# Self-attention scores of a head pair as alternating 64-row products, with the projections issued in halves

## The chip, the core and the metric

The kernel runs on one core of a Trainium2 chip. The metric is the device time of one execution in microseconds (us), median of three runs. Engine names are those of the profile: PE is the matrix engine (PEld its weight loads, which can overlap its products), DVE the vector engine, ACT the scalar (activation) engine, POOL and SP the general and the DMA-issuing engine. PSUM is the accumulator memory of PE, 8 banks of 128 rows by 512 fp32 numbers.

## What is computed

A decoder layer on x of 8 batches of 512 tokens by 512: a windowed self-attention with 16 heads of 64, then a cross-attention, then a routed feed-forward block. Only the first part is touched by the change. Its core in the reference is:

```python
def proj(w):
    return jnp.einsum('bsd,de->bse', h, w).reshape(B, S, H, HD).transpose(0, 2, 1, 3)
q, k, v = (proj(w_q), proj(w_k), proj(w_v))
...
ll = jnp.einsum('bhnqd,bhnkd->bhnqk', qw, kw) * scale
cm = jnp.tril(jnp.ones((W, W), bool))
ll = jnp.where(cm, ll, NEG).reshape(B, H, S, W)
...
attn = jax.nn.softmax(jnp.concatenate([ll, lg], axis=-1), axis=-1)
```

The kernel handles one window of 512 tokens (one batch) at a time. The extra "gathered" keys of the reference are the same tokens again, so they enter as a weight of 1 or 2 on each value row (`twice`).

## The kernel before

**Precision.** Projections and scores need more than one fp32r product can give, so each operand is split into a high part (rounded to fp32r) and a low part (the rest), and a product is high x high + low x high + high x low. For the projections that is `product` (L577, L578, L579), three 128-row products of 512 columns for each of four chunks `c`, so 12 for one q or k of a head pair.

**Tiles of a head pair.** A pair p holds two heads: head 0 in rows 0 to 63, head 1 in rows 64 to 127 of the projection's bank. Before the change q goes into `q_both` and k into `k_twice` and `k_lo`. For each head, `q_both` has the high part of q in the head's own 64 rows and the low part in the other 64 rows; `k_twice` has the high part of k in both halves. So one 128-row product (L661, L659) does high x high and low x high at once, and one 64-row product with `k_lo` (L664, L657) adds the third term. A product with a bf16 identity (L665) adds the causal mask to the diagonal 128 columns.

**Units.** A pair's scores fall into five units (`unit_blocks`), each of 512 columns: u=0 and u=1 are the query tile 3 (512 keys) of head 0 and head 1; u=2 and u=3 are query tiles 0 and 2 (128 and 384 keys) of either head; u=4 is query tile 1 (256 keys) of both heads. Unit number i is 5p + u, 40 in a batch. Unit i of the scores is written to `s_bank[i % 2]`.

**Life of a unit.** PE computes the scores ("s"). DVE takes the row maximum (`nmax`, L530, L525). ACT takes the exponential into `probs` (L405) and counts `p_ready`. PE transposes the 128x128 blocks ("t", L673). DVE copies them to `probs_t` (L538). PE multiplies by the values ("pv", L688, eight recorded products of 65 columns). DVE divides by the sum (L552, L553) into `o_norm`. After a pair, "ot" (L697) transposes `o_norm`, and ACT copies it to `o_t`.

**What sets the order.** One list, `attention_plan`, is walked by every engine in the same order, and each engine does in order the steps in which it has work. In step g, before the change, the list holds s(g), t(g-2), pv(g-3), and for u = 0 to 3 one of q, q_lo, k, k_lo of the next pair: "q" and "k" are the projection on PE and the high copy on ACT; "q_lo" and "k_lo" are the subtraction on DVE. Some steps carry work for the next batch on DVE: "stats" (g = 5), "dot" (g = 14), "rank" (g = 22, 24, 27, 29). Engines wait for each other through counting semaphores. PE's scores of unit i wait only for the exponential of unit i-2, which freed its bank:

```python
if i >= 2:
    pe.wait_ge(p_ready, b * NU + i - 1)
```

The eight batches are a hardware loop. Values (v) are projected first in each batch, eight times 12 products, and the last two of them stand behind the first pair's q and k to cover their copies. The last pair of a batch has no next pair to project.

Of the kernel before, what the change touches and what calls it, by code (L numbers as in the profile page):

```python
# [18 lines left out]
F32 = mybir.dt.float32  # L19
# [9 lines left out]
P = 128  # L29
# [49 lines left out]

def head_rows(h):  # L80

    return slice(HD * h, HD * h + HD)


def attention_plan():
# [7 lines left out]
    plan = [("v", i) for i in range(2 * TT - 2)] + [("q", 0), ("q_lo", 0), ("k", 0), ("k_lo", 0)]  # L93
    plan += [("v", i) for i in range(2 * TT - 2, 2 * TT)]
    for g in range(NU + 7):
        p, u = divmod(g, UNITS)
        if g < NU:
            plan.append(("s", g))
# [4 lines left out]
        if g < NU and p + 1 < NPAIR and u < 4:  # L103
            plan.append((("q", "q_lo", "k", "k_lo")[u], p + 1))
# [22 lines left out]
def self_attention(nc, x, norm_w, w_q, w_k, w_v, w_out, scorer_w, scorer_b, x1):  # L127
# [3 lines left out]
    with ExitStack() as ctx:  # L131
# [17 lines left out]
        q_both, k_twice = sb("q_both", [P, 2, 2, S], F32R), sb("k_twice", [P, 2, 2, S], F32R)  # L149
        k_lo = sb("k_lo", [P, 2, S], F32R)  # L150
# [42 lines left out]
        s_ready, s_half = sem("s_ready"), sem("s_half")  # L193
# [24 lines left out]
        def taken(eng, b, key):  # L218
# [139 lines left out]
        def _(act):  # L358
# [16 lines left out]
            with act.Fori(0, B) as b:  # L375
                for kind, i in plan:
# [21 lines left out]
                    if kind == "s":  # L398
# [5 lines left out]
                        for n, (_, _, c0, nk) in enumerate(unit_blocks(i % UNITS)):  # L404
                            ins = nc.scalar.activation(probs[:, i % 2, c0:c0 + nk], s_bank[i % 2][:, c0:c0 + nk],  # L405
# [10 lines left out]
        def _(dv):  # L416
# [83 lines left out]
            with dv.Fori(0, B) as b, done.loop(b, 2 * TT + 2 * TT + 1 + NU, B):  # L500
                for kind, i in plan:
# [6 lines left out]
                    if kind in ("q_lo", "k_lo"):  # L508
                        slot, _ = pj(b, (kind[0], i))
                        dv.wait_ge(qk_hi, b * (2 * NPAIR) + 2 * i + (1 if kind == "q_lo" else 2))  # L510
                        for h in range(2):
                            own, other = head_rows(h), head_rows(1 - h)
                            if kind == "q_lo":
                                ins = nc.vector.scalar_tensor_tensor(q_both[other, i % 2, h, :], pj_bank[slot][own, :],  # L514
                                                                     HD ** -0.5, q_both[own, i % 2, h, :].bitcast(F32),
                                                                     ALU.mult, ALU.subtract)
                            else:
                                ins = nc.vector.tensor_tensor(k_lo[own, i % 2, :], pj_bank[slot][own, :],
                                                              k_twice[own, i % 2, h, :].bitcast(F32), ALU.subtract)
                        ins.then_inc(qk_lo, 1)  # L520
                    if kind == "s":
                        dv.wait_ge(s_ready, b * NU + i + 1)
                        blocks = unit_blocks(i % UNITS)
                        if i % UNITS == UNITS - 1:
                            ins = nc.vector.tensor_reduce(nmax[:, i % 4, :],  # L525
                                                          s_bank[i % 2][:, :].rearrange("p (h k) -> p h k", h=2),
                                                          AX.X, ALU.max, negate=True)
                        else:
                            for n, (_, _, c0, nk) in enumerate(blocks):
                                ins = nc.vector.tensor_reduce(nmax[:, i % 4, n:n + 1], s_bank[i % 2][:, c0:c0 + nk],  # L530
                                                              AX.X, ALU.max, negate=True)
# [42 lines left out]
        def _(pe):  # L574
# [46 lines left out]
            with pe.Fori(0, B) as b:  # L621
                for kind, i in plan:
# [13 lines left out]
                    if kind in ("q", "k"):  # L636
                        slot, _ = pj(b, (kind, i))
                        pe.wait_ge(split_lo, 4 if i < NPAIR // 2 else 6)
                        pj_empty(b, (kind, i))
                        for c in range(DC):  # L640
                            ins = product(pj_bank[slot][:, :], w_hi[kind][:, c, P * i:P * i + P],
                                          w_lo[kind][:, c, P * i:P * i + P], ht_hi[:, c, :], ht_lo[:, c, :],
                                          c == 0, c == DC - 1)
                        ins.then_inc(pj_ready, 1)
                    if kind == "s":
                        p, u = divmod(i, UNITS)
                        slot = i % 2
                        if u == 0:
                            pe.wait_ge(qk_lo, b * (2 * NPAIR) + 2 * p + 2)
                        if i >= 2:  # L650
                            pe.wait_ge(p_ready, b * NU + i - 1)
                        for h, t, c0, nk in unit_blocks(u):
                            queries, rows = slice(P * t, P * t + P), head_rows(h)
# [1108 lines left out]
```

## Time and profile before

| what | value |
|---|---|
| runs | 2414.29, 2414.99, 2419.1 us; median 2414.99 |
| span of the profiled execution | 2414.0 us (the runs add at least 0.3 us around it) |
| PE busy | 2241.6 us, 93% of the span |
| DVE busy | 1349.6 us, 56% |
| ACT busy | 845.5 us, 35% |
| self-attention | about the first 1650 us, eight batches of some 201 us |

The span runs from the first to the last recorded instruction; it is the number against which sums are made. Busy time of PE is modelled: a recorded product of 512 columns lasts 0.39 us while the next one starts 0.23 us after it, so the cost of a product is read from the start of one to the start of the next.

### The profile page before, as it was taken

To read this page: it belongs to the slowest core of one execution; us is meant where nothing else is said; L and a number is where in the kernel's file an instruction comes from. 1 tells how busy PE (TensorE), PEld (TensorE's weight loads), DVE (VectorE), ACT (ScalarE), POOL (GpSimd) and SP (SyncE) were. 2 spreads that over 40 slices of the span, in tenths; PEclk is the share of its full clock that TensorE was granted. 3 is DMA by queue.
4 is the path that set the end of the run, shared out by engine and by line. 5 is a ranking of instruction groups with operands and counts; after the bars stand their busy time and mean duration, and the time that the engine had idled before them with its cause. 6 is when DMAs were issued, how large, how long until landed. Compare 5 with 4: busy or idle time off the path is not lost. (4 is left out here: it accounts for less than half of the span.)

```text
span 2414.0 us, 35686 instructions
## 1 busy us (share of the span) xinstructions
PE 2241.6 (93%) x12029; PEld 1682.4 (70%) x12029; DVE 1349.6 (56%) x3145; ACT 845.5 (35%) x1541; POOL 429.2 (18%) x669
## 2 busy tenths in 40 slices
PE   3999999999999999999999999996898888878899
PEld 3786777678678677767767767773787888865543
DVE  4574376177257437617725743661787878845500
ACT  3442344144144234314414423441644444413210
POOL 2100000010010000001001000002866666620000
PEclk9999999999999999999999999997988888858999
DMA  5000000100100000010010000002013211141000
GB/s 183 1 1 31 23 1 10 45 1 1 54 1 1 31 23 1 10 45 1 1 54 1 1 28 27 1 10 91 29 56 102 83 55 55 53 152 50 1 0 18
DMA packets 46136, 80.23 MB, mean 33 GB/s; under 512 B 10067, under 2 KB 10067, under 8 KB 45448
## 3 DMA queue, kind: packets, MB, share of 16 engines
q1 hardware_dynamic: 45320, 75.85, 9.3%
q8 instruction: 103, 1.69, 0.3%
q0 software_dynamic: 640, 2.10, 0.2%
q14 instruction: 73, 0.60, 0.1%
HBM read 60.11 MB, written 17.83 MB: 32 GB/s over the span
## 5 line engine op out<-in xcount | busy, mean ns | idle before, releaser
L405 ACT ACTIVATE probs<-s_bank,nmax 128x512 f32<-128x512 f32 (+3 forms) x512 | 249.4, 525 | 421.6 <-DVE nmax L530 294.3
L530 DVE TENSOR_REDUCE nmax<-s_bank 128x1 f32<-128x512 f32 (+2 forms) x384 | 185.3, 510 | 305.7 <-PE s_bank L665 302.0
L688 PE MATMUL o_bank<-vals,probs_t 128*128 128x65 f32 x2560 | 322.2, 269 | 0.0
L688 PEld LDWEIGHTS o_bank<-vals,probs_t 128*128 128x128 f32 x2560 | 311.0, 192 | 1.4 <-DVE probs_t L538 1.4
L712 PE MATMUL pj_bank<-w_o,o_t 128*128 128x512 f32 x512 | 223.5, 597 | 6.0 <-ACT o_t L413 6.0
L538 DVE COPY probs_t<-pt_bank 128x512 f32<-128x512 f32 x320 | 218.0, 681 | 3.6 <-PE pt_bank L673 3.6
L319 POOL TENSOR_TENSOR idle<-ones 128x4 f32<-128x4 f32 x41 | 8.1, 198 | 1065.7 <-DMA probs<-in_x 1063.7
L673 PE MATMUL pt_bank<-ident,probs 128*128 128x128 f32 x1280 | 194.1, 274 | 0.0
L712 PEld LDWEIGHTS pj_bank<-w_o,o_t 128*128 128x128 f32 x512 | 97.2, 191 | 127.6 <-issue 127.6
L664 PE MATMUL s_bank<-k_lo,q_both 64*128 64x512 f32 (+3 forms) x448 | 184.9, 413 | 0.0
L514 DVE SCALAR_TENSOR_TENSOR q_both<-pj_bank,q_both 64x512 fp32r<-64x512 f32 x128 | 88.2, 689 | 141.6 <-ACT q_both L392 138.9
L661 PE MATMUL s_bank<-k_twice,q_both 128*128 128x512 f32 (+3 forms) x448 | 166.9, 373 | 0.0
L383 ACT ACTIVATE vals<-pj_bank,twice 128x512 f32<-128x512 f32 x64 | 43.9, 688 | 341.8 <-PE pj_bank L579 336.5
L1259 PEld LDWEIGHTS x_o_bank<-vx,p_t 77*128 77x128 f32 x1024 | 148.9, 224 | 17.2 <-issue 10.0
L1259 PE MATMUL x_o_bank<-vx,p_t 77*128 77x33 f32 x1024 | 143.8, 300 | 3.9 <-DVE att L1141 3.9
L570 DVE TENSOR_TENSOR probs<-pj_bank,probs 128x512 f32<-128x512 f32 x32 | 22.1, 692 | 213.8 <-PE pj_bank L712 195.3
L664 PEld LDWEIGHTS s_bank<-k_lo,q_both 64*128 64x128 f32 x448 | 81.9, 183 | 85.5 <-issue 72.1
L673 PEld LDWEIGHTS pt_bank<-ident,probs 128*128 128x128 f32 x1280 | 135.7, 141 | 0.0
L577 PE MATMUL pj_bank<-wv_hi,ht_hi 128*128 128x512 f32 x256 | 104.2, 407 | 22.9 <-ACT vals L383 9.9
L1245 PE MATMUL e_bank<-qk_bd,xl_t 128*128 128x308 f32 x256 | 96.9, 510 | 27.7 <-DVE e L1123 27.0
L1022 POOL TENSOR_TENSOR e<-e,fill 128x616 f32<-128x616 f32 x64 | 95.3, 1489 | 127.1 <-DVE fill L1129 126.9
L665 PE MATMUL s_bank<-causal_b,ident_b 128*128 128x128 bf16 x512 | 117.7, 230 | 0.0
(266 smaller groups left out, 4245.5 us busy)
## 6 DMA issues: line engine op xcount, KB each, us to landing
xb<-in_x SPq DMA_DIRECT2D x9, 1024.0 KB, 5.3
xt<-x SPq DMA_DIRECT2D x36, 256.0 KB, 2.8
probs<-in_x SPq DMA_DIRECT2D x32, 256.0 KB, 2.7
x<-probs SPq DMA_DIRECT2D x32, 256.0 KB, 2.0
am<-in_L_ffn_attention_mask SPq DMA_DIRECT2D x8, 1024.0 KB, 5.2
out<-x SPq DMA_DIRECT2D x32, 256.0 KB, 2.1
w_sb<-in_L_ffn_w SPq DMA_DIRECT2D x2, 4096.0 KB, 20.2
o_t<-in_L_attn_w_v SPq DMA_DIRECT2D x2, 1024.0 KB, 9.5
```

The source lines that it names most:

```text
L405: ins = nc.scalar.activation(probs[:, i % 2, c0:c0 + nk], s_bank[i % 2][:, c0:c0 + nk], ACT.Exp, bias=nmax[:, i % 4, n:n + 1])
L530: ins = nc.vector.tensor_reduce(nmax[:, i % 4, n:n + 1], s_bank[i % 2][:, c0:c0 + nk], AX.X, ALU.max, negate=True)
L538: nc.vector.tensor_copy(probs_t[:, i % 2, :], pt_bank[slot][:, :]).then_inc(ts_ready, 1)
L577: nc.tensor.matmul(out, lhs_hi, rhs_hi, start=start, stop=False)
L661: nc.tensor.matmul(s_bank[slot][:, c0:c0 + nk], *high, start=True, stop=False)
L664: nc.tensor.matmul(s_bank[slot][:, c0:c0 + nk], *low, start=False, stop=False)
L665: ins = nc.tensor.matmul(s_bank[slot][:, c0 + nk - P:c0 + nk], ident_b[:, :], causal_b[:, :], start=False, stop=True)
L673: ins = nc.tensor.transpose(pt_bank[slot][:, P * j:P * j + P], probs[:, i % 2, P * j:P * j + P], ident[:, :])
L688: ins = nc.tensor.matmul(o_bank[slot][:, o0:o0 + VW], probs_t[:, i % 2, c0 + P * kt:c0 + P * kt + P], vals[:, kt, 2 * p + h, :], start=(kt ...
L712: ins = nc.tensor.matmul(pj_bank[slot][:, :], o_t[:, c, P * i:P * i + P], w_o[:, c, :], start=(c == 0), stop=(c == NPAIR - 1))
L1245: ins = nc.tensor.matmul(e_bank[:, c, 0:CH * SK], xl_t[:, (i // 2) % 2, P * k:P * k + P], qk_bd[:, n.par, k].rearrange("p h k -> p (h k)") ...
L1259: ins = nc.tensor.matmul(o_bank[:, VX * h:VX * h + VX], p_t[:, i % 2, h // CH, P * (h % CH):P * (h % CH) + P], vx[:, n.par, 2 * CH * (i % ...
```

## The change

The plain tiles `q_hi`, `q_lo`, `k_hi`, `k_lo` (both heads in their own 64 rows) replace `q_both` and `k_twice`. One copy of 128 rows on ACT and one subtraction of 128 rows on DVE replace the 64-row ones (for q two and two, for k four and two). The scores become three 64-row products for each block and head (high x high, low x high, high x low). They are issued in turn for head 0 (rows 0 to 63, into `s_bank[0]`) and head 1 (rows 64 to 127, into `s_bank[1]`). A step "rows" does the scores of two units at once (j=0: units u=0, 1; j=1: u=2, 3), or of unit 4 (j=2), and waits until both banks are free. The projections of the next pair are issued as four steps of six products.

```diff
+def row_blocks(j):
+
+    return [[(3, 0, 512)], [(0, 0, 128), (2, 128, 384)], [(1, 0, 256)]][j]
...
     for g in range(NU + 7):
         p, u = divmod(g, UNITS)
-        if g < NU:
-            plan.append(("s", g))
+        more = g < NU and p + 1 < NPAIR
         if 2 <= g < NU + 2:
             plan.append(("t", g - 2))
         if 3 <= g < NU + 3:
             plan.append(("pv", g - 3))
-        if g < NU and p + 1 < NPAIR and u < 4:
-            plan.append((("q", "q_lo", "k", "k_lo")[u], p + 1))
+        if g < NU and u in (0, 2):
+            plan.append(("rows", 3 * p + u // 2))
+        if more and u == 3:
+            plan.append(("k", p + 1))
+        if g < NU and u == 3:
+            plan.append(("rows", 3 * p + 2))
+        if g < NU:
+            plan.append(("s", g))
+        if more and u < 3:
+            plan.append((("q_half", "q", "k_half")[u], p + 1))
+        if more and u == 2:
+            plan.append(("q_lo", p + 1))
+        if more and u == 4:
+            plan.append(("k_lo", p + 1))
...
+        def scores(i, n, c0, nk):
+
+            if i % UNITS == UNITS - 1:
+                return s_bank[n][:, 0:nk]
+            return s_bank[i % UNITS % 2][:, c0:c0 + nk]
...
-                        for h in range(2):
-                            own, other = head_rows(h), head_rows(1 - h)
-                            if kind == "q":
-                                ins = nc.scalar.activation(q_both[own, i % 2, h, :], pj_bank[slot][own, :], ACT.Copy,
-                                                           scale=HD ** -0.5)
-                            else:
-                                nc.scalar.copy(k_twice[own, i % 2, h, :], pj_bank[slot][own, :])
-                                ins = nc.scalar.copy(k_twice[other, i % 2, h, :], pj_bank[slot][own, :])
-                        ins.then_inc(qk_hi, 1)
+                        if kind == "q":
+                            nc.scalar.activation(q_hi[:, i % 2, :], pj_bank[slot][:, :], ACT.Copy,
+                                                 scale=HD ** -0.5).then_inc(qk_hi, 1)
+                        else:
+                            nc.scalar.copy(k_hi[:, i % 2, :], pj_bank[slot][:, :]).then_inc(qk_hi, 1)
...
+                    if kind in ("q_half", "q", "k_half", "k"):
+                        of = kind[0]
+                        slot, _ = pj(b, (of, i))
+                        if kind == of:
+                            chunks = range(DC // 2, DC)
+                        else:
+                            chunks = range(DC // 2)
...
+                    if kind == "rows":
+                        p, j = divmod(i, 3)
+                        first = UNITS * p + 2 * j
+                        if j == 0:
                             pe.wait_ge(qk_lo, b * (2 * NPAIR) + 2 * p + 2)
...
+                        if first:
+                            pe.wait_ge(p_ready, b * NU + first)
+                        blocks = row_blocks(j)
+                        terms = ((q_hi, k_hi), (q_lo, k_hi), (q_hi, k_lo))
+                        for n, (t, c0, nk) in enumerate(blocks):
+                            for m, (queries, keys) in enumerate(terms):
+                                for h in range(2):
+                                    nc.tensor.matmul(s_bank[h][:, c0:c0 + nk],
+                                                     queries[head_rows(h), p % 2, P * t:P * t + P],
+                                                     keys[head_rows(h), p % 2, 0:nk],
+                                                     start=(n == 0 and m == 0), stop=False, skip_group_check=True)
+                        for h in range(2):
+                            for n, (t, c0, nk) in enumerate(blocks):
+                                ins = nc.tensor.matmul(s_bank[h][:, c0 + nk - P:c0 + nk], ident_b[:, :],
+                                                       causal_b[:, :], start=False, stop=(n == len(blocks) - 1),
+                                                       skip_group_check=True)
+                            if j < 2 or h == 1:
+                                ins.then_inc(s_ready, 1)
```

**PE, before, in the middle of a pair**, from the last products of k's projection (L577 to L579) over unit u=3 to its t and pv (line numbers of the kernel before):

```order
L577 MATMUL pj_bank<-ht_hi,wk_hi 128x512
L578 MATMUL pj_bank<-ht_hi,wk_lo 128x512
L579 MATMUL pj_bank<-ht_lo,wk_hi 128x512
L651 REGISTER_ALU
L661 MATMUL s_bank<-k_twice,q_both 128x128 [waits p_ready]
L664 MATMUL s_bank<-k_lo,q_both 128x128
L665 MATMUL s_bank<-causal_b,ident_b 128x128
L661 MATMUL s_bank<-k_twice,q_both 128x384
L664 MATMUL s_bank<-k_lo,q_both 128x384
L665 MATMUL s_bank<-causal_b,ident_b 128x128
L673 MATMUL pt_bank<-ident,probs 128x128 [waits ts_ready,p_ready]
L673 MATMUL pt_bank<-ident,probs 128x128 x3
```

The same place of the change, with its own line numbers: L586 to L588 are `product`, L672 the 64-row products, L678 the mask, L688 the transposes.

```order
L586 MATMUL pj_bank<-ht_hi,wk_hi 128x512
L587 MATMUL pj_bank<-ht_hi,wk_lo 128x512
L588 MATMUL pj_bank<-ht_lo,wk_hi 128x512
L666 REGISTER_ALU
L672 MATMUL s_bank<-k_hi,q_hi 128x256 [waits p_ready]
L672 MATMUL s_bank<-k_hi,q_hi 128x256
L672 MATMUL s_bank<-k_hi,q_lo 128x256 x2
L672 MATMUL s_bank<-k_lo,q_hi 128x256 x2
L678 MATMUL s_bank<-causal_b,ident_b 128x128 x2
L685 REGISTER_ALU
L688 MATMUL pt_bank<-ident,probs 128x128 [waits ts_ready,p_ready]
L688 MATMUL pt_bank<-ident,probs 128x128 x3
```

What stood behind k's projection was unit 5p+3, whose bank the exponential of 5p+1 had freed; now it is unit 5p+4, which needs both banks, so it waits for the exponential of 5p+3.

**ACT, before, at the same place**: the copies of k (L395, L396), then the exponentials of unit 5p+3 (L405, 128 and 384 columns).

```order
L395 CAST k_twice<-pj_bank 64x512 [waits pj_ready]
L396 CAST k_twice<-pj_bank 64x512
L395 CAST k_twice<-pj_bank 64x512
L396 CAST k_twice<-pj_bank 64x512
L399 REGISTER_ALU
L403 REGISTER_ALU [waits max_ready]
L405 ACTIVATE probs<-s_bank,nmax 128x128 [waits pt_ready]
L405 ACTIVATE probs<-s_bank,nmax 128x384
```

And in the change (L415 is the copy of k, L423 the exponential):

```order
L410 REGISTER_ALU
L415 CAST k_hi<-pj_bank 128x512 [waits pj_ready]
L417 REGISTER_ALU
L421 REGISTER_ALU [waits max_ready]
L423 ACTIVATE probs<-s_bank,nmax 128x128 [waits pt_ready]
L423 ACTIVATE probs<-s_bank,nmax 128x384
```

The four copies became one; its place ahead of the exponentials of unit 5p+3 is the same as before.

**DVE, in the change, around unit 5p+4**: the copy of a transposed unit (L547), the division (L561, L562), then the maxima of unit 5p+4 (L539, 256 columns from either bank) and the low part of k (L533).

```order
L544 REGISTER_ALU
L547 COPY probs_t<-pt_bank 128x512 [waits pv_ready,pt_ready]
L561 RECIPROCAL o_rden<-o_bank 128x1 [waits pv_ready]
L65 REGISTER_ALU
L562 TENSOR_TENSOR o_norm<-o_bank,o_rden 128x64 [waits dve_step]
L537 REGISTER_ALU
L539 TENSOR_REDUCE nmax<-s_bank 128x1 [waits s_ready]
L539 TENSOR_REDUCE nmax<-s_bank 128x1
L528 REGISTER_ALU
L533 TENSOR_TENSOR k_lo<-pj_bank,k_hi 128x512 [waits qk_hi]
```

Before the change a step's maximum stood ahead of its copy and division; now t(g-2) and pv(g-3) of the step come first, and the maxima of unit g behind them.

## Rows read from the trace of the kernel before

**Rows 1.** The page, busy time of PE, share of the span, instructions.

```profile
PE 2241.6 (93%) x12029; PEld 1682.4 (70%) x12029; DVE 1349.6 (56%) x3145; ACT 845.5 (35%) x1541; POOL 429.2 (18%) x669
```

**Rows 2.** Busy time in one pair's 18 us of self-attention (window; length, engines; clock).

```profile
321.00:339.00 18.00, 18.00 (x113) 14.34 (x113) 13.98 (x35) 7.84 (x16) 0.00 (x0) 1.00 0.01 1
```

**Rows 3.** Timeline of PE, one pair: start, duration, line, operation, tiles, count.

```profile
508.53 0.48 PE L661 MATMUL s_bank<-k_twice,q_both 128*128 128x512 f32 x1
508.94 0.49 PE L664 MATMUL s_bank<-k_lo,q_both 64*128 64x512 f32 x1
509.37 0.23 PE L665 MATMUL s_bank<-causal_b,ident_b 128*128 128x128 bf16 x1
509.44 0.61 PE L673 MATMUL pt_bank<-ident,probs 128*128 128x128 f32 x4
509.88 1.00 PE L688 MATMUL o_bank<-vals,probs_t 128*128 128x65 f32 x8
510.69 0.48 PE L577 MATMUL pj_bank<-ht_hi,wq_hi 128*128 128x512 f32 x1
...
513.54 0.39 PE L661 MATMUL s_bank<-k_twice,q_both 128*128 128x512 f32 x1
...
514.35 0.61 PE L673 MATMUL pt_bank<-ident,probs 128*128 128x128 f32 x4
...
515.60 0.31 PE L661 MATMUL s_bank<-k_twice,q_both 128*128 128x128 f32 x1
...
516.92 0.61 PE L673 MATMUL pt_bank<-ident,probs 128*128 128x128 f32 x4
...
521.03 0.22 PE L661 MATMUL s_bank<-k_twice,q_both 128*128 128x128 f32 x1
...
522.25 0.61 PE L673 MATMUL pt_bank<-ident,probs 128*128 128x128 f32 x4
...
523.63 0.38 PE L657 MATMUL s_bank<-k_lo,q_both 64*128 64x256 f32 x1
...
524.88 0.60 PE L673 MATMUL pt_bank<-ident,probs 128*128 128x128 f32 x4
...
526.53 0.48 PE L661 MATMUL s_bank<-k_twice,q_both 128*128 128x512 f32 x1
```

**Rows 4.** Timeline of ACT in the same pair.

```profile
518.65 0.84 ACT L405 ACTIVATE probs<-s_bank,nmax 128x128 f32<-128x128 f32 x2 [2.61 <-DVE nmax L530]
521.23 0.58 ACT L395 CAST k_twice<-pj_bank 64x512 fp32r<-64x512 f32 x1 [1.74 <-PE pj_bank L579]
```

**Rows 5.** Timeline of DVE in the same pair.

```profile
509.63 0.69 DVE L530 TENSOR_REDUCE nmax<-s_bank 128x1 f32<-128x512 f32 x1 [0.51 <-PE s_bank L665]
...
517.78 0.76 DVE L530 TENSOR_REDUCE nmax<-s_bank 128x1 f32<-128x128 f32 x2
...
523.83 0.17 DVE L552 RECIPROCAL o_rden<-o_bank 128x1 f32<-128x1 f32 x1
524.03 0.23 DVE L553 TENSOR_TENSOR o_norm<-o_bank,o_rden 128x64 f32<-128x64 f32 x1
524.17 1.38 DVE L518 TENSOR_TENSOR k_lo<-pj_bank,k_twice 64x512 fp32r<-64x512 f32 x2
```

**Rows 6.** Timeline of DVE, the step "stats" in another pair.

```profile
292.34 2.46 DVE L426 BATCH_NORM_STATS2 bn<-xb 128x6 f32<-128x512 f32 x4
```

**Rows 7.** Waits of PE: total us, times, longest.

```profile
PE pj_bank L577 <- DVE k_lo L518: 6.9, 8, 0.9
```

**Rows 8.** Two idle times of PE in the cross-attention (timeline), and windows around them.

```profile
1727.28 1.10 PE L1252 MATMUL x_pt_bank<-x_ident,e 128*77 128x128 f32 x8 [1.32 <-ACT e L1077]
1748.51 0.63 PE L1238 MATMUL t_bank<-x_ident,xl 128*128 128x128 f32 x4 [2.22 <-ACT vx L1058]
...
1726.00:1732.00 6.00, 4.72 (x39) 4.45 (x40) 4.97 (x12) 4.22 (x8) 5.76 (x9) 1.00 0.15 46
1750.00:1753.00 3.00, 3.00 (x12) 2.28 (x10) 0.74 (x3) 2.38 (x4) 1.26 (x5) 0.53 0.00 0
```

More of the change, by code:

```diff
@@ L85, in attention_plan @@
 def attention_plan():
-    plan = [("v", i) for i in range(2 * TT - 2)] + [("q", 0), ("q_lo", 0), ("k", 0), ("k_lo", 0)]
+    plan = [("v", i) for i in range(2 * TT - 2)]
+    plan += [("q_half", 0), ("q", 0), ("q_lo", 0), ("k_half", 0), ("k", 0), ("k_lo", 0)]
     plan += [("v", i) for i in range(2 * TT - 2, 2 * TT)]
@@ L146, in self_attention @@
         vals = sb("vals", [P, TT, H, VW])
-        q_both, k_twice = sb("q_both", [P, 2, 2, S], F32R), sb("k_twice", [P, 2, 2, S], F32R)
-        k_lo = sb("k_lo", [P, 2, S], F32R)
+        q_hi, q_lo, k_hi, k_lo = (sb(n, [P, 2, S], F32R) for n in ("q_hi", "q_lo", "k_hi", "k_lo"))
         probs = sb("probs", [P, 2, 512])
@@ L192, in self_attention @@
         v_ready, v_sum_ready, qk_hi, qk_lo = sem("v_ready"), sem("v_sum_ready"), sem("qk_hi"), sem("qk_lo")
-        s_ready, s_half = sem("s_ready"), sem("s_half")
+        s_ready = sem("s_ready")
         max_ready, p_ready = sem("max_ready"), sem("p_ready")
@@ L404, in _ @@
                         for n, (_, _, c0, nk) in enumerate(unit_blocks(i % UNITS)):
-                            ins = nc.scalar.activation(probs[:, i % 2, c0:c0 + nk], s_bank[i % 2][:, c0:c0 + nk],
+                            ins = nc.scalar.activation(probs[:, i % 2, c0:c0 + nk], scores(i, n, c0, nk),
                                                        ACT.Exp, bias=nmax[:, i % 4, n:n + 1])
@@ L510, in _ @@
                         dv.wait_ge(qk_hi, b * (2 * NPAIR) + 2 * i + (1 if kind == "q_lo" else 2))
[L511 to L519, printed above, removed]
+                        if kind == "q_lo":
+                            ins = nc.vector.scalar_tensor_tensor(q_lo[:, i % 2, :], pj_bank[slot][:, :], HD ** -0.5,
+                                                                 q_hi[:, i % 2, :].bitcast(F32), ALU.mult, ALU.subtract)
+                        else:
+                            ins = nc.vector.tensor_tensor(k_lo[:, i % 2, :], pj_bank[slot][:, :],
+                                                          k_hi[:, i % 2, :].bitcast(F32), ALU.subtract)
                         ins.then_inc(qk_lo, 1)
@@ L522, in _ @@
                         dv.wait_ge(s_ready, b * NU + i + 1)
[L523 to L526, printed above, removed]
+                        for n, (_, _, c0, nk) in enumerate(unit_blocks(i % UNITS)):
+                            ins = nc.vector.tensor_reduce(nmax[:, i % 4, n:n + 1], scores(i, n, c0, nk),
                                                           AX.X, ALU.max, negate=True)
[L528 to L531, printed above, removed]
                         ins.then_inc(max_ready, 1)
@@ L635, in _ @@
                         ins.then_inc(pj_ready, 1)
[L636 to L642, printed above, removed]
-                                          c == 0, c == DC - 1)
-                        ins.then_inc(pj_ready, 1)
@@ new lines, in _ @@
+                    if kind in ("q_half", "q", "k_half", "k"):
[3 more added lines that the diff above has]
+                            chunks = range(DC // 2, DC)
+                        else:
+                            chunks = range(DC // 2)
+                            pe.wait_ge(split_lo, 4 if i < NPAIR // 2 else 6)
+                            pj_empty(b, (of, i))
+                        for c in chunks:
+                            ins = product(pj_bank[slot][:, :], w_hi[of][:, c, P * i:P * i + P],
+                                          w_lo[of][:, c, P * i:P * i + P], ht_hi[:, c, :], ht_lo[:, c, :],
+                                          c == 0, c == DC - 1)
+                        if kind == of:
+                            ins.then_inc(pj_ready, 1)
```

22 lines of the change are left out of this document (removed).

## The prediction

> **What bounds the kernel now.** I read the page first: PE is busy 93% of the span, DVE 56%, ACT 35% [rows 1]. Then the windows: in a pair's 18 us of self-attention PE is busy all 18.00, DVE 13.98, ACT 7.84, at the full clock [rows 2]. So PE sets the time there, and DVE and ACT have slack on average. Then PE's timeline of one pair, from one unit u=0 to the next: 508.53 to 526.53 is 18.00 us [rows 3]. What the change must be judged by is therefore two things: how much PE time the scores lose, and whether the new order makes PE wait, which it does not do now.
>
> **What the scores cost PE now.** From a unit's first product to the next transposes [rows 3]: u=0 takes 0.91 us (508.53 to 509.44), u=1 0.81, u=2 1.32, u=3 1.22, u=4 1.25, together 5.51 us a pair. Much of that is not streaming. Twelve projection products take 2.85 us (510.69 to 513.54), 0.24 us each, of which I take 0.23 for one in the middle. But the 128-row score product is followed only after 0.41 us by the 64-row one, and that only after 0.43 us by the mask. So going from 128 to 64 rows costs about 0.18 us and coming back 0.20 us. The mask itself costs 0.07 us. Each of the eight blocks of a pair pays both changes of row height; after the change each of the three groups pays them once.
>
> **What they cost after.** A group has pairs of 64-row products, one for either head. No row here shows two 64-row products on different halves in turn. Bounds for such a pair are one stream (0.23 us for 512 columns) and two. The nearest row is the 128-row product: it feeds both halves with 512 columns at once in 0.23 us, so I take one stream. A floor is the weight load: eight products of only 65 columns follow each other in 0.81 us (509.88 to 510.69), 0.10 us each, and I take that as the time of one load [rows 3]. Two loads a pair make 0.20 us, more than the stream of 128, 256 or 384 columns (0.06, 0.12, 0.18 us). Then:
>
> - j=0: 0.18 in, 0.23 + 0.23, last pair 0.43 with the way out, two masks 0.14: 1.21 us.
> - j=1: 0.18, three pairs of 128 columns 0.60, two of 384 columns 0.40, the last 0.18 + 0.20, four masks 0.28: 1.84 us.
> - j=2: 0.18, two pairs 0.40, the last 0.12 + 0.20, two masks 0.14: 1.04 us.
>
> Together 4.09 us, so 1.42 us a pair are saved. Lower bound: no load floor and no cost on the way in give 2.9 us (saving 2.6). Upper bound, the two halves one after the other: 1.90 + 2.34 + 1.24 = 5.48 us (saving nothing).
>
> The Trainium skill, TensorEngine Tiling (Array Packing), section Key Properties, says that different tiles can load weights and multiply in parallel. No run here shows it yet; by it the groups would come near the 2.9 us, and that is a rival below.
>
> **The new wait A, ahead of unit 4.** The scores of 5p+4 stand directly behind the second half of k's projection and need both banks, so the exponential of 5p+3. ACT does the copy of k ahead of that exponential, and that copy needs the end of k's projection. So PE waits for work that could only start when PE had finished. Take E as the moment at which PE could go on. ACT starts a copy 0.20 us after that (521.03 to 521.23), the copy takes 0.58 us for 512 columns, the two exponentials (128 and 384 columns) 0.84 us [rows 3, 4]. ACT to PE has no row here; I take the 0.11 us that lie between the maxima's end (517.78 + 0.76) and the exponential at 518.65 [rows 4, 5]. Sum: 1.73 us of idle PE in each pair but the last of a batch. Behind the waiting product stand t and pv of 5p+2, so DVE and then everything else of the next step is late too. Without the copy in the way there would still be a wait: pv(5p) ends on PE 1.43 us (half a k) before E, and behind it come 0.19 to DVE, 0.34 for the division, 0.76 for the maxima, 0.11, 0.84 and 0.11, so E + 0.92.
>
> **The new wait B, ahead of the next pair.** From the end R of unit 4's scores PE has t, pv, ot, t, pv: 1.65 us (524.88 to 526.53 has just t, pv, ot) plus 1.25, so 2.90 us. The next group needs the exponential of 5p+4. DVE's list puts copy and division of the earlier units first: pv(5p+1) ends for PE at R + 1.25, DVE starts 0.19 us later (509.44 to 509.63), the division holds it 0.34 us (523.83 to 524.17), two maxima 0.76, 0.11 to ACT, two exponentials 0.84, 0.11 back: R + 3.60. PE idles 0.70 us; in the first pair, which has no ot (0.40 us), 1.10 us [rows 3 to 5]. The low part of k follows the maxima on DVE and ends at about R + 3.2, in time. Between j=0 and j=1 the same walk leaves 0.5 us of slack: PE has two half projections, two t (0.44) and two pv (0.81), 5.4 us; its first pv there ends after 2.7, and 0.19, 0.4 for a division of two, 0.69 for the maxima of 512 columns, 0.11, as much as the maxima for the exponential, and 0.11 make 4.9. No DMA and no work of POOL is added or moved.
>
> **Smaller terms, per batch.** "Stats" delays DVE by 2.46 us [rows 6] and by 0.4 more that I take for its small instructions, exactly between j=0 and j=1 of the second pair, where 0.5 us is spare: the walk gives +0.9 us. "Dot", also four passes over 512 columns, gives +0.4. The ranks fall on slack. The last pair has no projections as filler; its waits grow to about what its groups save: +0.2. Against that, the values' last projection waits 0.86 us for k_lo now (6.9 us in 8 times) [rows 7]; with one copy of 0.58 instead of four, and one subtraction instead of two, it no longer does: -0.9. Cheaper copies gain nothing elsewhere, since neither ACT nor DVE was waited for. Halving the projections costs PE two more starts a pair, some 0.08 us each, which I set against the exposed load at unit 4's start today.
>
> **Sum.** A usual pair: 1.73 + 0.70 - 1.42 = +1.01 us. A batch: six of these 6.1, the first pair 1.4, the last 0.2, stats and dot 1.3, values -0.9: +8.1 us; eight batches: +65 us. The span of 2414.0 becomes 2479, and 2480 with the 1 us by which the runs' median lies above the span; for this case alone 2440 to 2510, since an error of 0.5 us in a pair's groups or waits is 28 us. Cross-attention and routed block are untouched.
>
> **The rivals.**
>
> *The halves run one after the other.* Then the groups take 5.48 us: +1.39 us a pair more, 56 pairs, +78 us: about 2558. For it: no row shows two products started together. Against it: the 128-row stream.
>
> *The clock falls in the waits.* In the cross-attention the clock stayed full (1.00) around an idle time of 1.32 us, and stood at 0.53, so mostly at the 1.2 GHz level, after one of 2.22 us [rows 8]. Wait A lies between (1.73 us, about 1.56 as recorded, since a record reaches 0.17 past the next start). If PE runs at 1.2 GHz for the 3 us behind it, t, pv and ot take about 1 us more that wait B cannot hide: 56 x 1 = +56 us, about 2536.
>
> *The groups are so short that they pay for the waits.* One mechanism: the loads of the two halves run side by side too, so the groups take 2.9 us, saving 1.2 us a pair more than I take. 56 x 1.2 = -67 us on the forecast: about 2413, and 2399 if the waits are 0.25 us shorter than walked. It decides at groups of about 2.95 us. For it: the load floor is taken from 128-row loads. Against it: even then only the waits' price is met, not beaten.
>
> *The change does not do what it says:* if each change of half costs what a change of row height does (0.18), the 24 products of a pair cost 4.3 us more than in a row: +240 us and beyond. Nothing in the trace shows such a cost between equal heights.
>
> **How the numbers follow.** Forecast 0.55; halves in turn 0.18; clock 0.12; short groups 0.11, of which faster than 0.2% below the median 0.08; halves with a change cost 0.04. A change within 0.2% (5 us) could not be told from none by three runs that spread over 5 us. The range 2428 to 2575 leaves out the fast end and the worst case. Faster 0.08, same 0.05 (the short groups' other part, and a forecast with all terms at their low ends), slower 0.87.
>
> **What the changed profile would show.** PE busy no longer all of a pair's window, but about 16.6 of 19 us; two waits of PE in each pair, on ACT's exponential, of about 1.6 and 0.6 us as recorded, 56 times each; the copy of k between them on ACT's timeline; groups of about 1.2, 1.8 and 1.0 us; the two halves' products starting almost together; no wait on k_lo at the values. The prediction is wrong if the groups take under 3 us, or if the exponential of 5p+3 ends before k's projection.

## The result, and the profile after

The changed kernel takes 2437.21 us (median of 5 runs, 2434.93 to 2448.78), the kernel before 2418.08 in the runs beside it (2414.29 to 2424.1). The ratio is 1.0091 [1.0067, 1.0116], so the change is slower by 0.9%, about 19 us. Forecast were 2480 us and some 65 us: the sign is right and the time is in the wide range (2428 to 2575), though 3 us below the 2440 to 2510 that the prediction gives for its own case, and the size is three times too large. The profiled run is the slowest of the five (2448.78 us, span 2447.1). Its last scores end 17.3 us later than before (1633.93 us after the start against 1616.62); the rest of the 33 us between the two spans lies mostly in later stages that the change doesn't touch, some 12 of them in the cross-attention, and I explain no more than the 19.

The page after, the row that answers to [rows 1]:

```profile
PE 2143.6 (88%) x12541; PEld 1654.9 (68%) x12541; DVE 1263.2 (52%) x3081; ACT 684.1 (28%) x1285; POOL 429.5 (18%) x669
```

The window of one pair, from one j=0 group to the next (length; busy time of PE, PEld, DVE, ACT, POOL; clock), against [rows 2]:

```profile
515.50:533.32 17.82, 16.00 (x120) 13.49 (x120) 9.99 (x26) 5.34 (x12) 0.00 (x0) 1.00 0.01 1
```

PE is busy 98 us less in the whole execution and now waits in every pair: 16.00 us of 17.82 are busy, where before all 18.00 were. The pair itself is no longer than before (17.82 against 18.00).

PE's timeline, the same stretch and the end of the pair ahead of it (start, duration, line, tiles, count; in brackets the idle time before). L672 are the 64-row products, L678 the mask, L688 the transposes, L586 a projection's first product. "x2" in an L672 row is the same product of both heads:

```profile
511.25 0.39 PE L672 MATMUL s_bank<-k_hi,q_hi 64*128 64x256 f32 x2 [1.42 <-ACT probs L423]
511.48 0.28 PE L672 MATMUL s_bank<-k_hi,q_lo 64*128 64x256 f32 x2
511.59 0.28 PE L672 MATMUL s_bank<-k_lo,q_hi 64*128 64x256 f32 x2
511.80 0.29 PE L678 MATMUL s_bank<-causal_b,ident_b 128*128 128x128 bf16 x2
511.93 0.61 PE L688 MATMUL pt_bank<-ident,probs 128*128 128x128 f32 x4
...
514.09 1.00 PE L703 MATMUL o_bank<-vals,probs_t 128*128 128x65 f32 x8
515.50 0.50 PE L672 MATMUL s_bank<-k_hi,q_hi 64*128 64x512 f32 x2 [0.41 <-ACT probs L423]
515.84 0.40 PE L672 MATMUL s_bank<-k_hi,q_lo 64*128 64x512 f32 x2
516.07 0.40 PE L672 MATMUL s_bank<-k_lo,q_hi 64*128 64x512 f32 x2
516.41 0.29 PE L678 MATMUL s_bank<-causal_b,ident_b 128*128 128x128 bf16 x2
516.50 0.47 PE L586 MATMUL pj_bank<-ht_hi,wq_hi 128*128 128x512 f32 x1
...
522.06 0.33 PE L672 MATMUL s_bank<-k_hi,q_hi 64*128 64x128 f32 x2
522.23 0.27 PE L672 MATMUL s_bank<-k_hi,q_lo 64*128 64x128 f32 x2
522.33 0.28 PE L672 MATMUL s_bank<-k_lo,q_hi 64*128 64x128 f32 x2
522.45 0.39 PE L672 MATMUL s_bank<-k_hi,q_hi 64*128 64x384 f32 x2
522.67 0.33 PE L672 MATMUL s_bank<-k_hi,q_lo 64*128 64x384 f32 x2
522.84 0.34 PE L672 MATMUL s_bank<-k_lo,q_hi 64*128 64x384 f32 x2
523.11 0.40 PE L678 MATMUL s_bank<-causal_b,ident_b 128*128 128x128 bf16 x4
523.32 0.48 PE L586 MATMUL pj_bank<-ht_hi,wk_hi 128*128 128x512 f32 x1
```

Read the distances between starts. Two products of 512 columns take 0.23 us together (515.84 to 516.07), what one 128-row product takes. Two of 128 columns take 0.10 to 0.12 us (522.23 to 522.33 to 522.45), two of 256 take 0.11 (511.48 to 511.59). The groups last 1.00, 1.26 and 0.68 us (to the next 128-row work at 516.50, 523.32 and 511.93): 2.94 us a pair instead of 5.51 [rows 3].

How PE comes to the wait ahead of unit 4, from the timelines of PE, DVE and ACT in another pair:

```profile
287.34 0.40 PE L588 MATMUL pj_bank<-ht_lo,wk_hi 128*128 128x512 f32 x1
...
286.67 0.74 DVE L539 TENSOR_REDUCE nmax<-s_bank 128x1 f32<-128x128 f32 x2
...
287.78 0.58 ACT L415 CAST k_hi<-pj_bank 128x512 fp32r<-128x512 f32 x1 [2.57 <-PE pj_bank L588]
288.26 0.84 ACT L423 ACTIVATE probs<-s_bank,nmax 128x128 f32<-128x128 f32 x2
...
289.16 0.39 PE L672 MATMUL s_bank<-k_hi,q_hi 64*128 64x256 f32 x2 [1.42 <-ACT probs L423]
```

The maxima of unit 5p+3 are done at 287.41. The exponential that the scores wait for starts only at 288.26, because ACT, idle for 2.57 us, is waiting for the end of k's projection and then copies k.

PE's waits in self-attention (total us, times, longest):

```profile
PE s_bank L672 <- ACT probs L423: 128.7, 133, 2.2
...
PE pt_bank L614 <- ACT o_t L431: 4.9, 7, 1.0
```

Neither row was there before. The wait of the values for k_lo [rows 7] is gone.

The last pair of a batch, from its j=0 group to the output projection: first the window before, then that of two batches after:

```profile
397.96:419.09 21.13, 19.18 (x144) 15.68 (x142) 14.79 (x37) 9.00 (x17) 1.85 (x4) 1.00 0.08 26
```

```profile
402.12:423.66 21.54, 15.91 (x137) 13.58 (x137) 13.49 (x35) 8.12 (x15) 1.89 (x4) 1.00 0.09 25
605.78:629.26 23.48, 18.84 (x136) 16.52 (x137) 13.60 (x35) 8.12 (x15) 1.85 (x4) 0.85 0.08 23
```

Three of the eight batches take 21.54 us here at the full clock; the other five take 22.6 to 23.5 at 0.85 to 0.93. The mean of the eight is 22.36.

So the time went as follows. Four pairs of a batch are 0.10 to 0.19 us shorter than before. The second ("stats") and the fourth ("dot") are 0.45 longer. The first pair and the last are longer too, and the stretch behind the last one is shorter. The ledger (the list of these differences with its sum) stands below, with the prediction's steps.

### The profile page after: what moved, and what is told of

Its sections match the earlier page's. It is cut to its first block and busy times, and to the rows that moved or that the text cites. A ratio compares the mean times of both kernels' runs of the same rounds, so it can differ in the third digit from the quotient of the medians.

```text
span 2447.1 us, 36390 instructions
## 1 busy us (share of the span) xinstructions
PE 2143.6 (88%) x12541; PEld 1654.9 (68%) x12541; DVE 1263.2 (52%) x3081; ACT 684.1 (28%) x1285; POOL 429.5 (18%) x669
## 3 DMA queue, kind: packets, MB, share of 16 engines
HBM read 60.11 MB, written 17.83 MB: 32 GB/s over the span
## 5 line engine op out<-in xcount | busy, mean ns | idle before, releaser
L423 ACT ACTIVATE probs<-s_bank,nmax 128x512 f32<-128x512 f32 (+3 forms) x512 | 248.2, 525 | 630.1 <-DVE nmax L539 617.6
L547 DVE COPY probs_t<-pt_bank 128x512 f32<-128x512 f32 x320 | 219.8, 687 | 253.3 <-PE pt_bank L688 248.5
L703 PE MATMUL o_bank<-vals,probs_t 128*128 128x65 f32 x2560 | 329.4, 273 | 3.0 <-DVE probs_t L547 3.0
L703 PEld LDWEIGHTS o_bank<-vals,probs_t 128*128 128x128 f32 x2560 | 317.9, 196 | 6.4 <-DVE probs_t L547 6.4
L539 DVE TENSOR_REDUCE nmax<-s_bank 128x1 f32<-128x512 f32 (+3 forms) x512 | 230.5, 483 | 115.2 <-PE s_bank L678 115.2
L672 PE MATMUL s_bank<-k_hi,q_hi 64*128 64x512 f32 (+3 forms) x512 | 103.0, 399 | 128.7 <-ACT probs L423 128.7
L688 PE MATMUL pt_bank<-ident,probs 128*128 128x128 f32 x1280 | 196.7, 277 | 1.9 <-ACT probs L423 1.9
L688 PEld LDWEIGHTS pt_bank<-ident,probs 128*128 128x128 f32 x1280 | 154.0, 143 | 24.1 <-ACT probs L423 3.0
L672 PEld LDWEIGHTS s_bank<-k_hi,q_hi 64*128 64x128 f32 x512 | 48.3, 185 | 170.6 <-ACT probs L423 163.5
L405 ACT ACTIVATE vals<-pj_bank,twice 128x512 f32<-128x512 f32 x64 | 43.9, 688 | 345.3 <-PE pj_bank L588 339.9
L579 DVE TENSOR_TENSOR probs<-pj_bank,probs 128x512 f32<-128x512 f32 x32 | 22.1, 692 | 213.8 <-PE pj_bank L727 207.6
L1260 PE MATMUL e_bank<-qk_bd,xl_t 128*128 128x308 f32 x256 | 104.6, 544 | 30.3 <-DVE e L1138 29.6
L586 PE MATMUL pj_bank<-wv_hi,ht_hi 128*128 128x512 f32 x256 | 102.5, 400 | 16.5 <-ACT vals L405 10.4
L530 DVE SCALAR_TENSOR_TENSOR q_lo<-pj_bank,q_hi 128x512 fp32r<-128x512 f32 x64 | 43.6, 682 | 135.2 <-ACT q_hi L412 135.2
L586 PE MATMUL pj_bank<-ht_hi,wk_hi 128*128 128x512 f32 x256 | 110.0, 430 | 0.0
L586 PE MATMUL pj_bank<-ht_hi,wq_hi 128*128 128x512 f32 x256 | 110.0, 430 | 0.0
```

Of the source, the lines that this page charges most:

```text
L423: ins = nc.scalar.activation(probs[:, i % 2, c0:c0 + nk], scores(i, n, c0, nk), ACT.Exp, bias=nmax[:, i % 4, n:n + 1])
L539: ins = nc.vector.tensor_reduce(nmax[:, i % 4, n:n + 1], scores(i, n, c0, nk), AX.X, ALU.max, negate=True)
L547: nc.vector.tensor_copy(probs_t[:, i % 2, :], pt_bank[slot][:, :]).then_inc(ts_ready, 1)
L586: nc.tensor.matmul(out, lhs_hi, rhs_hi, start=start, stop=False)
L672: nc.tensor.matmul(s_bank[h][:, c0:c0 + nk], queries[head_rows(h), p % 2, P * t:P * t + P], keys[head_rows(h), p % 2, 0:nk], start=(n == 0 ...
L688: ins = nc.tensor.transpose(pt_bank[slot][:, P * j:P * j + P], probs[:, i % 2, P * j:P * j + P], ident[:, :])
```

## The experiments

The expectations speak of theory 1, formed from the rows above. The two halves of TensorE run their products and their loads side by side, so a pair of heads needs 2.94 us of score time. This gain is paid away in two waits of a pair, about 1.6 and 0.6 us from start to start, that the order of the steps makes, not the 64-row products. It expects that where a wait goes, its full length comes back. The rival in each case is that what the edit touches is not on the path, so that the time stays near the 2437 us of the changed kernel, for the reason that the text gives. Ratios are to the kernel before on the same chip; its medians there were 2415.57 and 2414.82 us.

### e6_same_half: both heads on one half

Both heads' products read the rows of head 0. This leaves out head 1's scores and computes head 0's twice, with the same number of products, columns and banks.

```diff
-  queries[head_rows(h), p % 2, P * t:P * t + P],
-  keys[head_rows(h), p % 2, 0:nk],
+  queries[head_rows(0), p % 2, P * t:P * t + P],
+  keys[head_rows(0), p % 2, 0:nk],
```

> Both products of each pair read head 0's rows 0 to 63, so head 1's scores are left out and head 0's computed twice; counts, sizes, banks and order stay. Theory 1 (two halves run side by side): on one half the products go one after the other, 0.23 us for 512 columns, 0.18 for 384, 0.11 for 256 and 128; the groups grow from 1.00, 1.26 and 0.68 by 0.69, 0.87 and 0.34, 1.9 us a pair, 64 pairs, +122 us, about 2559. Theory 2 (the groups are short only because they change row height once): no change, 2437.

Measured: 2600.83 us (2594.76 to 2609.61), ratio 1.0775 [1.0747, 1.0802]. PE's timeline, the starts of a j=1 and a j=2 group:

```profile
528.72 0.44 PE L672 MATMUL s_bank<-k_hi,q_hi 64*128 64x128 f32 x2
529.00 0.38 PE L672 MATMUL s_bank<-k_hi,q_lo 64*128 64x128 f32 x2
529.22 0.38 PE L672 MATMUL s_bank<-k_lo,q_hi 64*128 64x128 f32 x2
...
536.64 0.50 PE L672 MATMUL s_bank<-k_hi,q_hi 64*128 64x256 f32 x2 [1.42 <-ACT probs L423]
536.98 0.40 PE L672 MATMUL s_bank<-k_hi,q_lo 64*128 64x256 f32 x2
```

Two products of 128 columns now take 0.22 us instead of 0.11, two of 256 take 0.34 at the group's start (536.64 to 536.98) instead of 0.23. A pair at the full clock takes 19.77 us instead of 17.82: 1.95 us, times 64 is 125 us, which makes 2562 of the 2601. In 44 of the 64 pairs the clock fell as well (a pair then takes 20.9 us or so instead of 19.77); the rest goes with that, though I did not add it up. Theory 1 holds: two products on different halves cost what one does, and that includes their loads, since two products of 128 columns take half as long on two halves as on one.

### e3_by_head: the same products, one head after the other

```diff
-  for n, (t, c0, nk) in enumerate(blocks):
-      for m, (queries, keys) in enumerate(terms):
-          for h in range(2):
+  for h in range(2):
+      for n, (t, c0, nk) in enumerate(blocks):
+          for m, (queries, keys) in enumerate(terms):
```

> In each group all products of head 0 are issued, then all of head 1, instead of in turn; nothing else. Theory 1 (two halves in turn run side by side, weight loads too): the groups grow from 1.00, 1.26 and 0.68 us by 0.46, 0.74 and 0.23, 1.4 us a pair, 64 pairs, +92 us, about 2529; products of 128 columns of one head follow each other at 0.10 us or more. Theory 2 (the groups are short because they change row height only once, and two 64-row products are no cheaper side by side): no change, 2437.

Measured: 2458.04 us (2457.13 to 2463.15), ratio 1.0166 [1.0141, 1.0191]: 21 us over the changed kernel, neither theory's number. PE's timeline, a j=0 group and the first half of a j=1 group (x1 is a product of one head; the x2 of the last row is head 1's first product and, 0.11 us later, head 0's first of 384 columns):

```profile
520.63 0.51 PE L672 MATMUL s_bank<-k_hi,q_hi 64*128 64x512 f32 x2 [0.41 <-ACT probs L423]
520.97 0.40 PE L672 MATMUL s_bank<-k_hi,q_lo 64*128 64x512 f32 x2
521.21 0.40 PE L672 MATMUL s_bank<-k_lo,q_hi 64*128 64x512 f32 x2
...
527.18 0.33 PE L672 MATMUL s_bank<-k_hi,q_hi 64*128 64x128 f32 x1
...
527.46 0.28 PE L672 MATMUL s_bank<-k_lo,q_hi 64*128 64x128 f32 x1
527.46 0.49 PE L672 MATMUL s_bank<-k_hi,q_hi 64*128 64x128 f32 x2
```

The j=0 group issues three products of head 0 and then three of head 1, and still they start two by two: products of the other half started beside products issued ahead of them. In the j=1 group, six and six, head 0 runs ahead for 0.28 us, and the group lasts 1.54 us instead of 1.26; this 0.3 us a pair, times 64, is about 19 of the 21 us. So different halves are what makes the overlap. The alternation in the issue, which the title names and which I had thought the cause, matters only for the long group.

### e1_k_late: the copy of k behind the exponential

ACT's copy of k becomes a step of its own, placed behind the scores of unit 5p+3 in the list, so that ACT does the exponential of 5p+3 first.

```diff
+  if more and u == 3:
+      plan.append(("k_copy", p + 1))
...
-  if kind in ("q", "k"):
+  if kind in ("q", "k_copy"):
```

> Only ACT's copy of k moves, behind the exponential of unit 5p+3. Theory 1 (wait A of 1.6 us a pair is set by that copy, which starts only when k's projection has ended): the wait falls to about 0.9 us, set by DVE's maxima behind pv(5p); 56 pairs x 0.7 = -39 us, about 2398 us. Theory 2 (the wait is set by DVE's order alone, the copy is hidden in it): no change, 2437.

Measured: 2413.30 us (2405.25 to 2418.24), ratio 0.9991 [0.9978, 1.0005]: 24 us under the changed kernel, not 39. ACT's and PE's timeline at the same place:

```profile
283.31 0.84 ACT L425 ACTIVATE probs<-s_bank,nmax 128x128 f32<-128x128 f32 x2 [2.33 <-DVE nmax L541]
284.04 0.59 ACT L417 CAST k_hi<-pj_bank 128x512 fp32r<-128x512 f32 x1
284.20 0.39 PE L674 MATMUL s_bank<-k_hi,q_hi 64*128 64x256 f32 x2 [0.68 <-ACT probs L425]
```

The exponential now follows the maxima, and the wait falls from 1.42 to about 0.7 us, so the copy did set its length. Pairs take 17.19 us where nothing else stood in the way. The fifth and sixth pair stayed at 17.87, and their wait at 1.45: there a "rank" step on DVE stands ahead of the maxima, which I had not counted.

### e2_max_first_u3, e5_max_first_u4, e7_max_first: scores ahead of t and pv in a step

In a step for unit g, DVE's maxima of g stand behind the copy and the division of units g-2 and g-3. These three kernels put ("s", g) ahead of ("t", g-2) and ("pv", g-3), at u=3, at u=4, and at u=1, 3 and 4; the cut is that of the first. On PE nothing moves, since its score groups stand under ("rows", j); DVE's maxima and ACT's exponentials come earlier, ahead of ACT's copy of k too.

```diff
+  early = g < NU and u in (3,)
+  if early:
+      plan.append(("s", g))
...
-  if g < NU:
+  if g < NU and not early:
       plan.append(("s", g))
```

> In step u=3 alone, maxima and exponential of unit 5p+3 stand ahead of t(5p+1), pv(5p) and the copy of k, on DVE and ACT. Theory 1 (the order of these steps makes wait A): the wait goes altogether, since the exponential is then back about 1.2 us before k's projection ends; 56 x 1.6 us and some 0.8 us in each batch's last pair, -96 us, about 2341. Theory 2 (the waits follow from needing both banks, whatever the order): the time moves into wait B, ahead of the next pair, and the sum stays within 10 us of 2437.

Measured: 2342.08 us (2340.85 to 2343.55), ratio 0.9689 [0.9665, 0.9713], theory 1's number. Its waits of PE:

```profile
PE s_bank L675 <- ACT probs L426: 49.5, 96, 1.1
```

The wait ahead of unit 4 is left in 24 of 64 pairs, those with ranks and the last of each batch. A pair takes 16.35 us, 1.45 less than after the change; the other wait keeps its 0.41 (0.85 behind the first pair).

> In step u=4 alone, maxima and exponential of unit 5p+4 stand ahead of t(5p+2) and pv(5p+1). Theory 1 (that order makes wait B): wait B, 0.41 us as recorded and 0.58 from start to start, 1.0 in a batch's first pair, goes; wait A stays at 1.42 as recorded; 49 x 0.58 + 7 x 1.0, -36 us, about 2401. Theory 2 (PE is held by k_lo or by the banks, not by DVE's order): no change, 2437.

Measured: 2414.33 us (2407.94 to 2422.23), ratio 1.0004 [0.9993, 1.0016]: 23 us of the expected 36. The wait ahead of the next pair is gone in all pairs; a usual one takes 17.38 us. That is some 0.46 us less than after the change, not the expected 0.58, so its length did not come back in full. Besides, the pair with "dot" gained nothing (18.87), and five pairs of the profiled run took 18.95 to 19.64 us where their like took 17.38 to 17.97; the clock was lower in them (0.91).

> Maxima and exponential first in steps u=1, 3 and 4. Theory 1 (the waits come from the order on DVE and ACT alone): both waits go in the usual pair, which falls to 18.0 - 2.6 saved in the scores, about 15.7 us with the further starts; from the 2342 of the run with u=3 alone another 36 for wait B and some 5 for the delay by the statistics: about 2300. Theory 2 (DVE as a whole is too late for groups of two banks): the waits move, no more than 10 us below 2342.

Measured: 2303.19 us (2301.8 to 2307.9), ratio 0.954 [0.9525, 0.9555], theory 1 again. It gains 134 us over the changed kernel, more than e2 (95) and e5 (23) together. Both waits are gone except for 24 of unit 4:

```profile
PE s_bank L675 <- ACT probs L426: 16.5, 24, 1.1
```

Usual pairs take 15.89 us, the two with ranks 16.4.

### e8_max_first_ranks: the ranks moved too

e7, and the "rank" steps of DVE one unit earlier in the two pairs that still waited.

```diff
-RANK_AT = (22, 24, 27, 29)
+RANK_AT = (21, 24, 26, 29)
```

> As the run with maxima first in u=1, 3 and 4, and the ranks of g=22 and 27 move to g=21 and 26, where DVE has slack. Theory 1 (the ranks' 1.5 us on DVE between the maxima of 5p+2 and 5p+3 keep 0.5 us of wait A in two pairs of a batch): 16 x 0.5 = -8 us against that run, about 2292. Theory 2 (they are hidden): the same as that run.

Measured: 2293.36 us (2292.0 to 2295.2), ratio 0.95 [0.9487, 0.9513], as expected: 5.0% under before and 5.9% under the changed kernel. A pair's window, and PE's waits:

```profile
474.47:490.30 15.83, 15.83 (x121) 13.46 (x120) 10.01 (x27) 5.67 (x11) 0.00 (x0) 1.00 0.01 2
```

```profile
PE s_bank L675 <- ACT probs L426: 9.1, 8, 1.1
```

PE is busy all of the pair again, as before the change, but for 15.83 us instead of 18.00. The eight waits left are those of the last pair of each batch.

### e4_whole_projections: the 64-row products without the halving

The projections are whole again, q's at u=0 and k's at u=2, so nothing of them lies between the units 3 and 4.

```diff
-  if more and u == 3:
-      plan.append(("k", p + 1))
...
-  if more and u < 3:
-      plan.append((("q_half", "q", "k_half")[u], p + 1))
+  if more and u in (0, 2):
+      plan += [("qk"[u // 2] + "_half", p + 1), ("qk"[u // 2], p + 1)]
```

> The projections are no longer split: all twelve products of q behind the first group of a pair, all of k behind the second, none ahead of the third. Theory 1 (the halves are cover, placed where PE would wait): the exponential of 5p+3 is awaited from the end of pv(5p), about 2.3 us instead of 1.6, and that of 5p+1 for about 0.9 us where it was covered; 56 x 1.6 = +90 us, about 2527. Theory 2 (the same products in fewer pieces change nothing, since PE waits for the same chains): within 15 us of 2437.

Measured: 2585.30 us (2582.56 to 2586.96), ratio 1.0691 [1.0664, 1.0718]. The halving is filler: without it the wait ahead of unit 4 is 2.13 to 2.22 us, and a third one of 0.70 stands at j=1. Both together lengthen a pair to 19.24 us (two pairs of the profiled run were about that short), 56 times 1.42 or 80 us. Most others take 20.4 us or more. PE's timeline behind such a wait, and windows around it:

```profile
527.30 0.58 PE L670 MATMUL s_bank<-k_hi,q_hi 64*128 64x256 f32 x2 [2.13 <-ACT probs L421]
...
529.28 1.81 PE L701 MATMUL o_bank<-vals,probs_t 128*128 128x65 f32 x8
```

```profile
527.00:530.00 3.00, 2.70 (x16) 2.48 (x17) 0.47 (x1) 0.24 (x1) 0.00 (x0) 0.53 0.02 5
530.00:533.00 3.00, 3.00 (x17) 3.00 (x16) 2.06 (x7) 0.67 (x2) 0.00 (x0) 0.50 0.00 0
```

The eight products of 65 columns take 1.81 us, recorded, instead of 1.00: the clock is at 0.50, the 1.2 GHz level. So the excess over the expected 2527 goes with the clock, which the expectation had not counted; its share was not measured by itself.

## Why the prediction was wrong in size

**The groups: the step that failed.** The prediction took 1.21 + 1.84 + 1.04 = 4.09 us; measured are 1.00 + 1.26 + 0.68 = 2.94. It had named groups of under 3 us as a sign that it is wrong. Two of its prices failed. The first was "A floor is the weight load ... Two loads a pair make 0.20 us". Two 64-row products on different halves take 0.11 us, loads included; e6 shows that 0.22 is the price on one half. By the rows that is 0.46 us of the error: 0.09 for each of the three pairs of 128 columns and the first two of 256, and nothing at the first two of 384, which take the 0.39 of 0.40 counted. The second was the change of row height, taken over from before as 0.18 and 0.20. It cost about 0.10 each way (the first pair of products of j=0 takes 0.34 us instead of 0.23, the last 0.34 too); over three groups that is 0.56 us of the error. The masks take 0.13 less than the 0.56 counted. Each price was taken from a 128-row neighbour or a single block; together they make the 1.15 us. For the way in, the trace before had a nearer row, at u=1 of the pair in [rows 3]:

```profile
513.86 0.49 PE L664 MATMUL s_bank<-k_lo,q_both 64*128 64x512 f32 x1
```

It follows the 128-row product of 513.54 after 0.32 us, 0.09 over the stream; at u=0, from which the 0.18 was taken, the 128-row product is itself the first behind shorter ones, and a projection's first product takes 0.08 us more in that place as well (510.69 to 511.00 instead of 0.23).

The lower bound of 2.9 us came out, and it had a chance of only 0.11. In part that is luck: it left out the way in, which costs some 0.3 us over three groups, and took a pair of 128 columns at 0.06 us instead of 0.11, but counted the way out and the masks too high by as much.

The Trainium skill, TensorEngine Tiling (Array Packing), section Key Properties, says that different tiles can load weights and multiply in parallel. The trace agrees, with 0.11 us for a pair of products against 0.22 on one half. The prediction named this rule as a rival and weighed it below a row that did not show two halves at all.

**The waits: right.** Wait A was walked as 1.73 us (1.56 as recorded); measured are 1.59 from start to start (289.16 less 287.34 and the 0.23 of the last product) and 1.42 recorded. Wait B was 0.70; measured are 0.60 (515.50 less 514.09 and 0.81) and 0.41 recorded. Both are there for the reason given: e1 shows the copy of k in wait A, e2, e5 and e7 that both vanish when the maxima and the exponential come first. "Without the copy in the way" the walk had left E + 0.92; e1 left 0.68 to 0.80 recorded, so 0.85 to 0.97 from start to start, outside the two pairs with ranks.

**A usual pair.** 1.59 + 0.60 - 2.57 = -0.38, and about 0.16 for two more projections' starts (a first product takes 0.31 us to the next instead of 0.23), which I had set against an exposed load: -0.22. Measured are -0.10 to -0.19 in the four pairs without an extra, -0.15 in the mean. The forecast was +1.01. This difference of 1.16 us, times 56, is 65 us, more than the 46 by which the forecast missed; the last pair gave 18 back.

**The smaller terms, per batch.** "Stats" and "dot" were to cost 0.9 and 0.4 over a usual pair; they cost 0.6 each (18.46 and 18.91 us against 18.01 and 18.45). By the figures that the prediction gives for "stats", 2.46 and 0.4 less 0.5, it would have been 2.4; how the 0.9 came about is not shown, so that term was near by luck. The first pair: 1.63 us longer, of which 1.25 is only that t and pv now stand ahead of the next pair's scores; the 0.38 left is 0.5 over a usual pair, forecast 0.4. From the output projection to the next batch's scores 1.37 us are saved: the 0.86 of k_lo, as said, and 0.5 that I did not trace.

**The last pair: wrong, and without it the change would come out about even.** The forecast was +0.2, since "its waits grow to about what its groups save". At the full clock the pair ends 0.41 us later (21.54 against 21.13) although the 1.25 us of t and pv have moved out of it, so it is 1.66 longer. Without projections as filler PE waits four more times, for the exponentials and for `o_t`; PE's timeline of the last pair, where brackets stand for a wait:

```profile
404.82 0.66 PE L688 MATMUL pt_bank<-ident,probs 128*128 128x128 f32 x4 [0.24 <-ACT probs L423]
...
406.56 0.33 PE L672 MATMUL s_bank<-k_hi,q_hi 64*128 64x128 f32 x2 [0.24 <-ACT probs L423]
...
411.53 0.38 PE L672 MATMUL s_bank<-k_hi,q_hi 64*128 64x256 f32 x2 [2.22 <-ACT probs L423]
...
416.34 0.63 PE L614 MATMUL pt_bank<-ident,xb 128*128 128x128 f32 x4 [0.98 <-ACT o_t L431]
```

These are 3.68 us as recorded and about 4.4 from start to start, against the 2.6 or 2.7 that the groups of this pair save. (The 0.41 ahead of its first group lies in the window of the pair before.) The order on DVE and ACT makes most of this too: with e7's order the last pair takes 19.00 us instead of 21.54. The fallen clock adds 0.82 in the mean (22.36 less 21.54).

**The ledger of a batch.** Six pairs of -0.15: -0.9; stats and dot +1.2; first pair +0.4; last pair +1.66 and +0.82; behind it -1.37; three other pairs in 64 with a fallen clock +0.3. Together +2.1 us, eight times 17. The ledger is that of the profiled execution, where the scores end 17.3 us later; the medians differ by 19. The forecast was +8.1.

**The rivals.** *Halves in turn* is excluded by e6 and by the 0.23 us of two 512-column products. *A cost for changing the half* is excluded by the same rows. *Short groups* was the right one, with the luck told above: it gave 2399 to 2413 with the waits 0.25 us shorter than walked or not, and they are 0.24 shorter. The measured 2437 lies above it by two terms that it took over unchanged from the forecast: the last pair (2.28 us more than +0.2, 18 us) and the projections' starts (0.16 times 56, 9 us). The 11 us left I did not split. *The clock* was real, but rare in the pairs that this rival meant: it fell in three of those 56, and besides in five of the eight last pairs, with their wait of 2.22 us. After most waits of 1.42 us it stayed full; where it fell, as here, PE's windows are

```profile
1209.00:1212.00 3.00, 1.58 (x18) 1.39 (x17) 0.20 (x1) 1.33 (x3) 0.00 (x0) 1.00 0.00 0
1212.00:1215.00 3.00, 3.00 (x19) 3.00 (x18) 2.71 (x7) 1.07 (x3) 0.00 (x0) 0.56 0.02 5
```

and the pair took 18.98 us instead of 17.83: the 1 us of that rival. e4 has it in nearly every pair. Why a wait of 1.42 us kept the clock in one pair and lost it in another stays open; no run here was made to tell it apart.

## What to carry to other kernels

Two products on the two halves of TensorE's rows cost one, loads and all, so charge such a pair once and do not take its floor from full-height neighbours. When a merged group needs both banks of a double buffer, walk the chain that frees the second bank and put its links (maximum, exponential) first in the lists of their engines, ahead of copies for later work: here that order was the difference between 0.9% slower and 5.0% faster. And look at a stretch without filler by itself: the last pair of a batch alone cost 2.28 us more than forecast, 18 us in all.

## What the runs showed of the hardware that was not expected

- Products on different halves overlap even when they are issued head by head: six products in the order 0,0,0,1,1,1 started two by two, 0.24 to 0.34 us apart (e3).
- Two 64-row products of 128 columns on different halves follow the next two after 0.11 us, on one half after 0.22 (after, e6).
- Recorded waits of 1.42 us mostly left the clock full (0.99 over 60 to 1500 us of the changed kernel); in e4, with waits of 2.13 to 2.22 us and others of 0.70, the same stretch had 0.93. Yet with the same waits of 1.42 us at unit 4, e6's clock was 0.95.
